# Row statistics moved from VectorE to ScalarE and the opening of an attention kernel put in another order

## The chip, the cores and the metric

The kernel runs on one core of a Trainium2 chip. The time is that of the device, in microseconds (us), for one launch. A core has five engines that work side by side, each through its own list of instructions in order: TensorE (PE in the profile, PEld for its weight loads), VectorE (DVE), ScalarE (ACT), GpSimd (POOL) and SyncE (SP), which here only issues DMAs. They wait for each other through semaphores.

## What is computed

Cross attention on a normalised input, with a residual, and behind it a transformer block with grouped-query attention over the four batches and a mixture of eight experts. The change touches only the opening of the first part:

```python
def _layernorm(x, axis=-1, eps=1e-05):
    m = jnp.mean(x, axis=axis, keepdims=True)
    v = jnp.var(x, axis=axis, keepdims=True)
    return (x - m) / jnp.sqrt(v + eps)
...
# B, S, D, H = (4, 512, 256, 16), DK = 16, 1024 context tokens
query = _rope(split_heads(q @ w_q.T))
key_ = _rope(split_heads(k @ w_k.T))
value = split_heads(v @ w_v.T)
scores = jnp.einsum('bhqd,bhkd->bhqk', query, key_) / np.sqrt(DK)
scores = jnp.where(mask[:, None, None, :] == 0, -10000.0, scores)
attn = jax.nn.softmax(scores, axis=-1)
...
x = x + _L0_xattn_ref(_layernorm(x, axis=-1), ctx_1024, ctx_1024, mask_BxS2_ik0, ...)
x = x + _L0_ffn_ref(_layernorm(x, axis=-1), ...)
```

x is (4, 512, 256), the context (4, 1024, 256), all in float32. Products are made exact enough by splitting both operands into a high and a low part (`_hi`, `_lo`) and adding three matmuls.

## The kernel before, in words

**Tiling.** The 2048 rows of x stand in SBUF as 16 tiles of 128 rows (`xt`, four to a batch). The attention of a batch goes in four quads of four heads; a quad has 8 groups, one for each 128 keys, so there are 128 groups in all. In a group TensorE computes scores for 4 heads (`score`, L974), ScalarE the exponentials (L643), and TensorE weighs the values (L989). Since the maximum of a row of scores has to be known ahead of its exponentials, each quad's scores are computed once more beforehand in the other orientation (`max`, L935: two matmuls of 49 rows into a `wide` bank) and VectorE reduces them (L781). There are 16 such maxima to a quad: 2 head pairs x 4 query tiles x 2 halves of the keys (`kh`). Then `nm` negates and joins them (L785 to L791), `mxt` turns them over (L940), ScalarE copies them to `mxp`, and SyncE's `load_max_rows` stores them as two more rows of `qst`.

**The order of the work.** `attention_order` writes one list of jobs; every engine walks it and does its own part of each job, so a place in the list fixes the order on all engines. The list `before` is the opening, up to the first group:

- ("rate", b): row statistics. VectorE's `statistics` does batch 0 at the very start, and batches 1 to 3 as ("rate", 1) behind the value projections of batch 0: 12 `bn_stats` (L700), 12 `bn_aggr` (L704), the variance plus epsilon (L706), then it waits for ScalarE's square root (L589) and makes `rstd` (L708) and `shift` (L711).
- ("xn", b, t): the normalised tile t, by ScalarE from batch 1 on (L608). ("xT", b): its transposes (L922), ScalarE's copy `xT_hi` (L637) and VectorE's subtraction `xT_lo` (L759). For batch 1 both stand in the opening, because its queries are projected from the second group on.
- ("c", b, g): GpSimd splits a half of the context (L521, L523). ("q"), ("k"), ("v"): projections (L849) and their evictions by ScalarE (L637); with an index at the end a job is a quarter of the work, 256 columns.
- ("rope", b, part): rotation of keys (part 0 and 1) or queries (part 2), by GpSimd or VectorE (L469 to L483).
- `first`, the 16 maxima of quad 0, upper half of the keys first: behind each of the first 12 stands one quarter job of batch 1, first the 8 of the keys, then 4 of the values. xT of batch 1 stands behind the eighth.
- Then `nm`, two value jobs, `mxt`, two maxima of quad 1, two value jobs, two more maxima; and then the groups. ScalarE loads the table for the exponential there (L660).

**Banks.** Maxima and transposes take turns on two `wide` banks, each freed by VectorE. Projections, `mxt` and scores go round in three `narrow` banks.

**SyncE's queue** is written by hand. Rotated pieces go to memory (`store_turned`, L353: `q_pieces` and `k_pieces`) and come back stacked for the heads (`load_queries` L374, `load_keys` L387). The first maximum waits for `quad_in`: the first two heads' queries and the upper half of their keys. A load waits for the landing of its store.

## Time and profile before

| | us |
|---|---|
| median of 3 runs | 776.78 |
| the three runs | 770.8, 776.78, 779.75 |
| the profiled execution | 778.03 |
| its span on the core | 776.2 |
| TensorE busy | 700.1 (90%) |
| VectorE busy | 559.5 (72%) |
| ScalarE busy | 494.4 (64%) |
| GpSimd busy | 355.3 (46%) |

### The profile page before, as it was taken

To read this page: it belongs to the slowest core of one execution; us is meant where nothing else is said; L and a number is where in the kernel's file an instruction comes from. 1 tells how busy PE (TensorE), PEld (TensorE's weight loads), DVE (VectorE), ACT (ScalarE), POOL (GpSimd) and SP (SyncE) were. 2 spreads that over 40 slices of the span, in tenths; PEclk is the share of its full clock that TensorE was granted. 3 is DMA by queue.
4 is the path that set the end of the run, shared out by engine and by line. 5 is a ranking of instruction groups with operands and counts; after the bars stand their busy time and mean duration, and the time that the engine had idled before them with its cause. 6 is when DMAs were issued, how large, how long until landed. Compare 5 with 4: busy or idle time off the path is not lost. (4 is left out here: it accounts for less than half of the span.)

```text
span 776.2 us, 13476 instructions
## 1 busy us (share of the span) xinstructions
PE 700.1 (90%) x4382; PEld 434.2 (56%) x4382; DVE 559.5 (72%) x919; ACT 494.4 (64%) x984; POOL 355.3 (46%) x262
## 2 busy tenths in 40 slices
PE   2379799999999999999999999889977789999996
PEld 2266444434344444444433433567766779999995
DVE  4995878888878878787988893367986435555553
ACT  2022367787777787878777778576646057677673
POOL 4857724880511096159668910000064703544444
PEclk9776699999999999999999999989987799999999
DMA  9575338667776474148967710089437636633321
GB/s 266 196 251 187 131 111 302 163 201 249 221 261 190 120 224 180 54 171 268 287 233 270 280 75 1 1 271 419 139 82 234 195 93 138 111 36 36 39 28 20
DMA packets 59719, 130.71 MB, mean 168 GB/s; under 512 B 8869, under 2 KB 26309, under 8 KB 58197
## 3 DMA queue, kind: packets, MB, share of 16 engines
q1 hardware_dynamic: 33364, 72.86, 27.9%
q0 software_dynamic: 16848, 35.95, 18.0%
q10 hardware_dynamic: 9440, 21.06, 9.2%
q8 instruction: 37, 0.61, 0.3%
q14 instruction: 30, 0.24, 0.1%
HBM read 80.80 MB, written 69.39 MB: 194 GB/s over the span
## 5 line engine op out<-in xcount | busy, mean ns | idle before, releaser
L781 DVE TENSOR_REDUCE mx<-wide 128x2 f32<-128x1024 f32 x256 | 307.3, 1222 | 62.5 <-PE wide L935 61.2
L643 ACT ACTIVATE probs<-narrow 128x512 f32<-128x512 f32 x492 | 265.6, 599 | 76.5 <-PE narrow L974 74.7
L974 PE MATMUL narrow<-qst,kst 51*128 51x512 f32 x492 | 186.5, 452 | 0.8 <-ACT probs L643 0.2
L935 PE MATMUL wide<-kst,qst 49*128 49x512 f32 x512 | 172.7, 466 | 9.0 <-DVE mx L781 6.4
L974 PEld LDWEIGHTS narrow<-qst,kst 51*128 51x128 f32 x492 | 79.8, 187 | 133.2 <-ACT probs L643 52.9
L989 PE MATMUL values<-probs,vaug 128*17 128x512 f32 x1024 | 136.4, 605 | 1.4 <-ACT probs L643 0.8
L1739 POOL DMA_INDIRECT out<-res,token x39 | 60.8, 1560 | 91.4 <-DMA out<-res,token 59.9
L935 PEld LDWEIGHTS wide<-kst,qst 49*128 49x128 f32 x512 | 71.3, 191 | 21.9 <-DVE mx L781 15.1
L1271 POOL DMA_DIRECT2D out<-xt x4 | 5.5, 1377 | 116.4 <-DVE xt L1466 116.4
L1764 ACT ACTIVATE h_hi<-narrow 128x512 fp32r<-128x512 f32 x39 | 23.4, 599 | 41.2 <-PE narrow L1844 41.2
L474 POOL TENSOR_TENSOR turn_b<-turn_a,tab 128x1024 f32<-128x1024 f32 x10 | 24.1, 2409 | 50.2 <-ACT turn_a L637 49.6
L1790 DVE TENSOR_TENSOR h_lo<-narrow,h_hi 128x512 fp32r<-128x512 f32 x39 | 27.0, 692 | 23.4 <-ACT h_hi L1764 23.4
L989 PEld LDWEIGHTS values<-probs,vaug 128*17 128x17 f32 x1024 | 17.0, 95 | 44.2 <-issue 27.0
L1278 POOL DMA_INDIRECT list_rows<-lists,rows_to x32 | 32.4, 1011 | 17.3 <-issue 8.5
L469 POOL TENSOR_SCALAR keep<-keep 128x512 f32<-128x512 int32 x7 | 13.6, 1945 | 54.1 <-ACT turn_a L637 50.8
L637 ACT ACTIVATE vaug<-narrow 128x256 f32<-128x256 f32 (+1 forms) x28 | 11.7, 416 | 41.8 <-PE narrow L849 40.9
L1786 DVE TENSOR_TENSOR y_lo<-y_full,y_hi 128x256 fp32r<-128x256 f32 x39 | 16.6, 425 | 29.1 <-ACT y_hi L1751 29.1
L1751 ACT ACTIVATE y_hi<-wide,lncol 128x128 fp32r<-128x128 f32 x78 | 36.3, 466 | 0.0
L1750 ACT ACTIVATE y_full<-wide,lncol 128x128 f32<-128x128 f32 x78 | 35.8, 459 | 0.1
L521 POOL CAST c_hi<-craw 128x1024 fp32r<-128x1024 f32 x5 | 5.2, 1039 | 57.1 <-DMA craw<-in_ctxT 36.1
L849 PE MATMUL narrow<-wv_hi,c_hi 128*128 128x256 f32 x64 | 17.5, 360 | 15.0 <-POOL wv_lo L486 15.0
L1835 PE MATMUL wide<-w_hi,y_hi 128*128 x78 | 28.2, 443 | 0.1
(291 smaller groups left out, 1371.6 us busy)
## 6 DMA issues: line engine op xcount, KB each, us to landing
list_rows<-in_w ACTq DMA_DIRECT2D x56, 342.0 KB, 5.5
kst<-k_pieces SPq DMA_DIRECT2D x14, 784.0 KB
k_pieces<-turn_a SPq DMA_DIRECT2D x16, 512.0 KB, 4.3
w_hi<-w_hi SPq DMA_DIRECT2D x16, 512.0 KB
w_lo<-w_lo SPq DMA_DIRECT2D x16, 512.0 KB
turn_a<-in_w POOLq DMA_DIRECT2D x11, 512.0 KB, 5.4
w_hi<-turn_b POOLq DMA_DIRECT2D x11, 512.0 KB, 2.9
w_lo<-turn_a POOLq DMA_DIRECT2D x11, 512.0 KB, 4.6
```

Of the source, the lines that this page charges most:

```text
L474: step(engine.tensor_tensor(z[:, :, :], a[:, :, :], cos, ALU.mult))
L643: nc.scalar.activation(probs[:, n % NP, :], score_bank(n), ACT.Exp, scale=DK ** -0.5).then_inc(exp_done, 1)
L781: last = nc.vector.tensor_reduce(mx[quad % 2][:, qt, :, hp, kh], slot[:, :, :], axis=AX.X, op=ALU.max)
L935: last = nc.tensor.matmul(slot[:, i, :], qst[u % 3][r:r + R_MAX, h, P * qt:P * qt + P], kst[u % 3][r:r + R_MAX, h, 512 * kh:512 * kh + 512 ...
L974: nc.tensor.matmul(score_bank(n), kst[u % 3][r:r + R_ALL, h, P * kt:P * kt + P], qst[u % 3][r:r + R_ALL, h, :], start=True, stop=True).the ...
L989: last = nc.tensor.matmul(values[32 * hq:32 * hq + DK + 1, :], vaug[b % 2][:, kt, h, :], probs[:, (4 * g + hq) % NP, :], start=kt == 0, st ...
L1278: pool.indirect_dma_start(list_dram, bass.IndirectOffsetOnAxis(rows_to[:, j, i, s:s + 1], 0), lists[j][:, i, s, :].bitcast(U32), None).the ...
L1739: pool.indirect_dma_start(out, bass.IndirectOffsetOnAxis(token[:, n:n + 1], 0), res[n % PIECES][:, :], None, bounds_check=TOKENS - 1, oob_ ...
L1750: nc.scalar.activation(yT[n % 2][:, k, :], y_banks[n % 2][:, k, :], ACT.Identity, **affine)
L1751: last = nc.scalar.activation(yT_hi[n % 2][:, k, :], y_banks[n % 2][:, k, :], ACT.Identity, **affine)
L1790: nc.vector.tensor_tensor(hT_lo[n % 2][:, :, :], h_banks[n % 2], hT_hi[n % 2][:, :, :].bitcast(F32), ALU.subtract).then_inc(h_lo_set, 1)
L1835: last = nc.tensor.matmul(up_banks[n % 2], a[n % 2][:, k, :], w[:, bass.ds(e, 1), k, :].rearrange("p e n -> p (e n)"), start=(i, k) == (0, ...
```

## The change

Four things in the opening, all of them order or place:

1. The statistics of batches 1 to 3 go to ScalarE, as a job ("sums", 1) behind the weight copies and ahead of the value projections of batch 0. For each of 12 tiles one pass sums the row (`accum_out`), one operation makes the negative means, and for each tile a second pass squares x plus this shift and sums. Each pass waits for the one before. The passes write their elements to a spare part of `attn`. VectorE keeps the variance, `rstd` and `shift` (`rest_of_statistics`). ScalarE's square root stays where ("rate", 1) stands.
2. ("xn", 1) goes behind the eighth key job, ("xT", 1) behind `mxt`.
3. The quarter jobs of batch 1 begin behind the third maximum and not behind the first.
4. SyncE stores the first half of the rotated keys behind the mask rows and the first queries' load, not ahead of them.

```diff
-    before += [("rate", 1), ("c", 1, 0), ("c", 1, 1)] + [("xn", 1, n) for n in range(QT)]
+    before += [("rate", 1), ("c", 1, 0), ("c", 1, 1)]
...
-        before += [j] + (keys + vals)[n:n + 1] * (n < 12) + [("rope", 1, 0)] * (n == 3) + [("rope", 1, 1)] * (n == 7) + [("xT", 1)] * (n == 7)
+        before += [j] + (keys + vals)[n - 2:n - 1] * (2 <= n < 14) + [("rope", 1, 0)] * (n == 5) + [("rope", 1, 1)] * (n == 9) + [("xn", 1, t) for t in range(QT)] * (n == 9)
...
         load_context(1, 0)
         store_turned(0, 2)
-        store_turned(0, 1)
         load_keep(1, 0)
         load_queries(0, slice(0, 2))
+        store_turned(0, 1)
         load_keys(0, slice(0, 2), (1,))
...
+            if kind == "sums":
+                for t in range(QT, NT):
+                    if t % QT == 0:
+                        act.wait_ge(x_in[t // QT], 16)
+                    nc.scalar.activation(attn[:, 3, :], xt[:, t, :], ACT.Copy, accum_out=sums[:, t:t + 1]).then_inc(act_step, 1)
+                    act.wait_ge(act_step, t - QT + 1)
+                n = NT - QT
+                nc.scalar.activation(shift[:, QT:], sums[:, QT:], ACT.Copy, scale=-1.0 / D).then_inc(act_step, 1)
+                act.wait_ge(act_step, n + 1)
+                for t in range(QT, NT):
+                    nc.scalar.activation(attn[:, 3, :], xt[:, t, :], ACT.Square, bias=shift[:, t:t + 1], accum_out=squares[:, t:t + 1]).then_inc(act_step, 1)
+                    act.wait_ge(act_step, n + 1 + t - QT + 1)
+                nc.scalar.activation(attn[:, 3, 0:1], shift[:, QT:QT + 1], ACT.Copy).then_inc(squares_set, 1)
+                return
...
-        def statistics(i, batches):
+        def rest_of_statistics():
+
+            dve.wait_ge(squares_set, 1)
+            nc.vector.tensor_scalar(varc[:, QT:], squares[:, QT:], 1.0 / D, EPS, ALU.mult, ALU.add).then_inc(var_set, 1)
+            dve.wait_ge(std_set, 2)
+            step(nc.vector.reciprocal(rstd[:, QT:], std[:, QT:]))
             settle()
+            nc.vector.tensor_tensor(shift[:, QT:], shift[:, QT:], rstd[:, QT:], ALU.mult).then_inc(shift_set, 1)
```

How the rows stand on the engines, from the program's order. ScalarE before, from its last weight copies to its last eviction ahead of the exponentials:

```order
L598 ACTIVATE wo_hi<-probs 128x512
L637 ACTIVATE vaug<-narrow 128x32x16 x4
L589 ACTIVATE std<-varc 128x12
L608 ACTIVATE xn<-xt,shift,rstd 128x256 x4
L637 ACTIVATE turn_a<-narrow 128x256 x8
L637 ACTIVATE xT_hi<-wide 128x1024
L637 ACTIVATE vaug<-narrow 128x16x16 x6
L637 ACTIVATE mxp<-narrow 8x512
L637 ACTIVATE vaug<-narrow 128x16x16 x2
```

and now (`turn_a` holds keys, `vaug` values, `stats` the sums):

```order
L614 ACTIVATE wo_hi<-probs 128x512
L596 ACTIVATE attn,stats<-xt 128x256 x12
L599 ACTIVATE shift<-stats 128x12
L602 ACTIVATE attn,stats<-xt,shift 128x256 x12
L604 ACTIVATE attn<-shift 128x1
L653 ACTIVATE vaug<-narrow 128x32x16 x4
L591 ACTIVATE std<-varc 128x12
L653 ACTIVATE turn_a<-narrow 128x256 x8
L624 ACTIVATE xn<-xt,shift,rstd 128x256 x4
L653 ACTIVATE vaug<-narrow 128x16x16 x6
L653 ACTIVATE mxp<-narrow 8x512
L653 ACTIVATE xT_hi<-wide 128x1024
```

The statistics' passes stand ahead of the first value evictions, the square root stays behind the fourth; `xn` moved behind the eight keys and `xT_hi` behind `mxp`.

SyncE before, from the store of the rotated queries to the first load of keys:

```order
L353 DMA q_pieces<-probs 128x2x512 x3
L353 DMA k_pieces<-turn_a 128x2x512
L353 DMA k_pieces<-turn_b 128x2x512
L353 DMA k_pieces<-turn_a 128x2x512
L342 DMA keep<-in_mask 128x512
L374 DMA qst<-q_pieces 48x1024 x2
L387 DMA kst<-k_pieces 49x2x512 x2
```

and now:

```order
L355 DMA q_pieces<-probs 128x2x512 x3
L344 DMA keep<-in_mask 128x512
L376 DMA qst<-q_pieces 48x1024 x2
L355 DMA k_pieces<-turn_a 128x2x512
L355 DMA k_pieces<-turn_b 128x2x512
L355 DMA k_pieces<-turn_a 128x2x512
L389 DMA kst<-k_pieces 49x2x512 x2
```

The three key stores moved behind three loads; the key load that waits for them still follows them.

TensorE before, from the last value projection of batch 0 on (`wide` banks hold maxima, `narrow` ones projections):

```order
L849 MATMUL narrow0<-wv_hi,c_lo1 128x256 x2
L935 MATMUL wide1<-kst0,qst0 128x512 x2
L849 MATMUL narrow1<-c_hi0,wk_hi 128x256 x2
L849 MATMUL narrow1<-c_lo0,wk_hi 128x256 x2
L849 MATMUL narrow1<-c_hi0,wk_lo 128x256 x2
L935 MATMUL wide0<-kst0,qst0 128x512 x2
L849 MATMUL narrow2<-c_hi0,wk_hi 128x256 x2
```

and now:

```order
L873 MATMUL narrow0<-wv_hi,c_lo1 128x256 x2
L959 MATMUL wide1<-kst0,qst0 128x512 x2
L959 MATMUL wide0<-kst0,qst0 128x512 x2
L959 MATMUL wide1<-kst0,qst0 128x512 x2
L873 MATMUL narrow1<-c_hi0,wk_hi 128x256 x2
L873 MATMUL narrow1<-c_lo0,wk_hi 128x256 x2
L873 MATMUL narrow1<-c_hi0,wk_lo 128x256 x2
L959 MATMUL wide0<-kst0,qst0 128x512 x2
```

Three maxima now come ahead of the first key projection. The third takes the bank of the first.

## Rows read from the trace of the kernel before

**Rows 1.** The page: busy tenths and granted TensorE clock in 40 equal slices.

```profile
PE   2379799999999999999999999889977789999996
...
PEclk9776699999999999999999999989987799999999
```

**Rows 2.** Busy time by stretches; the column behind POOL is the granted clock.

```profile
core 0: us, PE busy (x) PEld busy (x) DVE busy (x) ACT busy (x) POOL busy (x), PEclk, DMA share, GB/s
...
56.00:68.00 12.00, 12.00 (x45) 8.69 (x44) 7.47 (x7) 2.65 (x8) 8.10 (x4) 0.51 0.71 207
...
76.50:80.80 4.30, 2.88 (x15) 1.55 (x14) 3.62 (x4) 0.77 (x2) 2.38 (x2) 0.90 0.05 18
80.80:90.00 9.20, 8.10 (x33) 6.15 (x34) 6.86 (x7) 1.74 (x4) 8.97 (x5) 0.50 0.05 18
...
200.00:300.00 100.00, 98.81 (x656) 44.62 (x656) 82.36 (x87) 77.95 (x151) 37.80 (x21) 1.00 0.64 196
```

**Rows 3.** Timeline at the seam: start us, us, engine, instruction, idle time before it.

```profile
83.06 0.19 DVE L785 TENSOR_REDUCE nm<-mx 128x16 f32<-128x32 f32 x1
...
85.55 1.01 PE L940 MATMUL narrow<-ident,mh 128*8 128x128 f32 x4 [1.08 <-DVE mh L791]
...
86.49 1.22 PE L935 MATMUL wide<-kst,qst 49*128 49x512 f32 x4
...
92.33 1.77 ACT L643 ACTIVATE probs<-narrow 128x512 f32<-128x512 f32 x3
```

**Rows 4.** Timelines of ScalarE, VectorE and GpSimd around the statistics.

```profile
43.79 0.60 ACT L637 ACTIVATE vaug<-narrow 128x512 f32<-128x512 f32 x1 [21.74 <-PE narrow L849]
...
45.98 4.01 DVE L700 BATCH_NORM_STATS2 stats<-xt 128x6 f32<-128x256 f32 x12
...
49.09 0.60 ACT L637 ACTIVATE vaug<-narrow 128x512 f32<-128x512 f32 x1 [0.83 <-PE narrow L849]
...
50.89 2.36 POOL L523 TENSOR_TENSOR c_lo<-xn,c_hi 128x1024 fp32r<-128x1024 f32 x1
...
50.97 2.31 DVE L706 TENSOR_SCALAR varc<-mv 128x12 f32<-128x12 f32 x1
...
53.31 0.21 ACT L589 ACTIVATE std<-varc 128x12 f32<-128x12 f32 x1 [3.63 <-DVE varc L706]
...
53.91 3.48 DVE L781 TENSOR_REDUCE mx<-wide 128x2 f32<-128x1024 f32 x3
...
54.11 2.08 ACT L608 ACTIVATE xn<-xt,shift,rstd 128x256 f32<-128x256 f32 x4 [0.58 <-DVE shift L711]
```

**Rows 5.** Timeline of TensorE: maxima of two pairs at each clock.

```profile
61.38 0.79 PE L935 MATMUL wide<-kst,qst 49*128 49x512 f32 x2
...
63.69 0.79 PE L935 MATMUL wide<-kst,qst 49*128 49x512 f32 x2
...
76.48 0.55 PE L935 MATMUL wide<-kst,qst 49*128 49x512 f32 x2
...
77.87 0.99 PE L935 MATMUL wide<-kst,qst 49*128 49x512 f32 x4
```

**Rows 6.** ScalarE's groups by form: count, busy us and mean ns.

```profile
L608 ACT ACTIVATE xn<-xt,shift,rstd 128x256 f32<-128x256 f32 x12 | 6.9, 597 | 0.6 <-DVE shift L711 0.6
```

**Rows 7.** Timeline of SyncE's issues, and the first maximum's weight load.

```profile
39.45 0.76 SPq L353 DMA_DIRECT2D k_pieces<-turn_a  x1
...
41.45 1.62 SPq L374 DMA_DIRECT2D qst<-q_pieces  x2
...
44.04 1.58 SPq L387 DMA_DIRECT2D kst<-k_pieces  x2
...
49.85 0.18 PEld L935 LDWEIGHTS wide<-kst,qst 49*128 49x128 f32 x2 [1.00 <-DMA kst<-k_pieces]
```

**Rows 8.** The tile kst up to 100 us: issue to landing.

```profile
DMA to landing us min/median/max: 6.3/7.7/12.1
```

**Rows 9.** Timeline of the turned rows of batch 1 (TensorE, VectorE).

```profile
68.15 1.84 PE L922 MATMUL wide<-ident,xn 128*128 128x128 f32 x8
...
71.16 1.23 DVE L759 TENSOR_TENSOR xT_lo<-wide,xT_hi 128x1024 fp32r<-128x1024 f32 x1 [3.11 <-ACT xT_hi L637]
```

More of the change, by code:

```diff
@@ L55, in attention_order @@
     before = [("rate", 0), ("xn", 0), ("w", "q"), ("c", 0, 1), ("w", "k"), ("mask", 0), ("xT", 0), ("k", 0, 1, 0), ("k", 0, 1, 1), ("rope", 0, 1), ("c", 0, 0),
-              ("q", 0, 0), ("q", 0, 1), ("rope", 0, 2), ("k", 0, 0, 0), ("k", 0, 0, 1), ("rope", 0, 0), ("w", "v"), ("w", "o")]
+              ("q", 0, 0), ("q", 0, 1), ("rope", 0, 2), ("k", 0, 0, 0), ("k", 0, 0, 1), ("rope", 0, 0), ("w", "v"), ("w", "o"), ("sums", 1)]
     before += [("v", 0, g, n) for g in range(2) for n in range(2)]
-    before += [("rate", 1), ("c", 1, 0), ("c", 1, 1)] + [("xn", 1, n) for n in range(QT)]
+    before += [("rate", 1), ("c", 1, 0), ("c", 1, 1)]
     keys, vals = [[(kind, 1, n // 4, n // 2 % 2, n % 2) for n in range(8)] for kind in "kv"]
@@ L61, in attention_order @@
     for n, j in enumerate(first):
-        before += [j] + (keys + vals)[n:n + 1] * (n < 12) + [("rope", 1, 0)] * (n == 3) + [("rope", 1, 1)] * (n == 7) + [("xT", 1)] * (n == 7)
-    before += [("nm", 0), vals[4], vals[5], ("mxt", 0)] + maxes(1)[:2] + vals[6:] + maxes(1)[2:AHEAD]
+        before += [j] + (keys + vals)[n - 2:n - 1] * (2 <= n < 14) + [("rope", 1, 0)] * (n == 5) + [("rope", 1, 1)] * (n == 9) + [("xn", 1, t) for t in range(QT)] * (n == 9)
+    before += [("nm", 0), vals[4], vals[5], ("mxt", 0), ("xT", 1)] + maxes(1)[:2] + vals[6:] + maxes(1)[2:AHEAD]
     timed = []
@@ L138, in cross_attention @@
     std = sb("std", [P, NT])
+    sums, squares = stats[:, :, 0], stats[:, :, 2]
     rstd = sb("rstd", [P, NT])
@@ L185, in cross_attention @@
     values_prepared, filled = sem("values_prepared"), sem("filled")
+    act_step, squares_set = sem("act_step"), sem("squares_set")
     var_set, std_set, shift_set = sem("var_set"), sem("std_set"), sem("shift_set")
@@ L693, in settle, with statistics @@
             dve.wait_ge(dve_step, steps[0])
-        def statistics(i, batches):
-            for b in batches:
-                dve.wait_ge(x_in[b], 16)
-                for t in range(QT * b, QT * b + QT):
-                    step(nc.vector.bn_stats(stats[:, t, :], xt[:, t, :]))
-            settle()
-            tiles = slice(QT * batches[0], QT * batches[-1] + QT)
-            for t in range(tiles.start, tiles.stop):
+        def rest_of_statistics():
[3 more added lines that the diff above has]
+            step(nc.vector.reciprocal(rstd[:, QT:], std[:, QT:]))
+            settle()
+            nc.vector.tensor_tensor(shift[:, QT:], shift[:, QT:], rstd[:, QT:], ALU.mult).then_inc(shift_set, 1)
+        def statistics():
+            dve.wait_ge(x_in[0], 16)
+            for t in range(QT):
+                step(nc.vector.bn_stats(stats[:, t, :], xt[:, t, :]))
+            settle()
+            for t in range(QT):
                 step(nc.vector.bn_aggr(mv[:, t, :], stats[:, t, :]))
             settle()
-            nc.vector.tensor_scalar_add(varc[:, tiles], mv[:, tiles, 1], EPS).then_inc(var_set, 1)
-            dve.wait_ge(std_set, i + 1)
-            step(nc.vector.reciprocal(rstd[:, tiles], std[:, tiles]))
+            nc.vector.tensor_scalar_add(varc[:, 0:QT], mv[:, 0:QT, 1], EPS).then_inc(var_set, 1)
+            dve.wait_ge(std_set, 1)
+            step(nc.vector.reciprocal(rstd[:, 0:QT], std[:, 0:QT]))
             settle()
-            if i > 0:
-                nc.vector.scalar_tensor_tensor(out=shift[:, tiles], in0=mv[:, tiles, 0], scalar=-1.0, in1=rstd[:, tiles], op0=ALU.mult, op1=ALU.mult).then_inc(shift_set, 1)
         def masks():
@@ L721, in _ @@
             if kind == "rate":
-                statistics(j[1], [0] if j[1] == 0 else list(range(1, B)))
+                if j[1] == 0:
+                    statistics()
+                else:
+                    rest_of_statistics()
                 continue
```

## The prediction

> **What bounds the kernel now.** I read the page first. Its slices [rows 1] show TensorE busy nine tenths or more from the sixth to the 25th, at full clock; the slices ahead of them are thinner, and the second to fifth have a lowered clock. The table by stretches [rows 2] says the same with numbers: from 200 to 300 us TensorE is busy for 98.81 of 100 us at clock 1.00. So the attention loop is TensorE's, it neither waits for the opening nor can catch up with it, and a microsecond won or lost ahead of the first exponential is one at the end. I therefore follow the opening alone, up to the first exponential at 92.33 us [rows 3], and let that move carry through one for one.
>
> Then the timeline of the opening. VectorE ends its last rope block at 46.0 and goes straight into the twelve row statistics of batches 1 to 3, and it isn't free for the first maximum before 53.91 [rows 4]. Of the 7.9 us between, 4.0 are the statistics, 1.0 the aggregation (until 50.97), and 2.31 one tiny operation on 12 columns, which began while GpSimd was in its 2.36 us subtraction (50.89 to 53.25) and ended 0.03 us after it. ScalarE stands idle for 21.74 us before the first value eviction at 43.79.
>
> From there the order on TensorE is maximum, projection, maximum, projection. One such pair takes 63.69 - 61.38 = 2.31 us at the low clock and 77.87 - 76.48 = 1.39 at the high one [rows 5]; a maximum without a projection costs VectorE 3.48 / 3 = 1.16 [rows 4]. From 56 to 68 us TensorE is busy for the whole 12.00 us and has 0.51 of its clock, that is 1.2 GHz; from 76.5 to 80.8 the same kind of work has 0.90 and from 80.8 to 90 again 0.50 [rows 2]. The clock, 0.92 us a pair, is the largest term in the opening, and nothing in the change sets it directly.
>
> **The change part by part.**
>
> Statistics to ScalarE. VectorE loses 12 statistics and 12 aggregations (5.0 us) and keeps three operations on 12 columns. ScalarE gets 12 sums, 12 squares and two tiny operations between its weight copies and its value evictions. The nearest row is the normalisation of the same 128x256 tiles, 597 ns [rows 6]. Each pass waits for the one before it, so I take 0.65: 24 x 0.65 + 0.5 = 16.1 us from 22.05, done at 38.2. No row has a sum read-out beside an activation. Bounds: 0.5 (the pitch of four overlapped ones, 2.08 / 4 [rows 4]) ends at 34.6, and twice the row, 1.2, ends at 51.3. At 0.65 the 21.74 us of idle time cover it with 5 us over, so it costs nothing; from 0.9 us a pass on it delays the value evictions.
>
> VectorE's first step then is early, but its reciprocal waits for the square root, and that stands on ScalarE behind the fourth value eviction: 49.09 + 0.60, + 0.21 for the root [rows 4], then 0.5 for reciprocal and shift: ready at 50.4. The shift is now a product of two operands in SBUF, and GpSimd works from 50.89 to 53.25 there. If the shift queues behind that, as the variance did, VectorE is ready at 53.5. Bounds 50.4 and 53.5; both gain on 53.91.
>
> The Trainium skill, "SBUF — State Buffer", section "Who interferes with whom", says that a VectorE instruction with two SBUF inputs, or in a two-port mode, blocks on a GpSimd instruction that reads SBUF until that one ends. The trace agrees with it at the 2.31 us operation, and by this rule the moved chain can still be held, until 53.25, and the first reduction then comes at 53.4 in place of the 53.2 below, which adds 0.2 us to the sum.
>
> The reordered loads. SyncE issues mask rows, then the first queries, and only then the key store of the first half. Before, store issues ended at 40.21 and mask and queries at 43.07 [rows 7]; swapped, the store ends 2.86 us later, at 43.07 (at best not at all later, if both fit into waits). The key load waits for this store to land: before 44.04 - 40.21 = 3.83 us, and the keys were there 49.85 - 44.04 = 5.81 us after its issue. So keys at 43.07 + 3.83 + 5.81 = 52.7, where they were at 49.85 with 3.6 us of slack ahead of VectorE. This eats nearly the whole gain: first maximum on TensorE at 52.7, reduction at 53.2 (bounds 50.9 and 55.1, the latter with the median landing of 7.7 [rows 8]). Gain 0.7 us.
>
> The store of the second half and everything behind it on SyncE's queue shift by little: its key load waits for its own store, and its first use is the ninth maximum.
>
> Order of the pairs. Before, two projections ran between the first two maxima while VectorE was still busy, so they were free, and four maxima at the end stood alone. Now the first two and the last two stand alone, and 12 pairs follow without a break. The third maximum needs the bank of the first: 53.2 + 1.2 = 54.4. All pairs low: 12 x 2.31 = 27.7, to 82.1. All high: 12 x 1.39 = 16.7, to 71.1. In the profile about half of the pairs behind the first ran low. I take 5 low and 7 high, 21.3, to 75.7. That is more high ones than before had because the row is unbroken: before, the turned rows in the middle left VectorE idle for 3.11 us and TensorE waiting, the gap in which a clock can fall [rows 9]. The last two maxima: 0.5 for TensorE and 2 x 1.2: 78.6, against 83.06 before [rows 3], 4.5 earlier. Here the bubble in the middle is gone too; it was 1.84 us of transposes, and the next maximum but one waited for the subtraction that ended at 71.16 + 1.23 [rows 9].
>
> The normalisation moves on ScalarE behind the eighth key eviction: 2.08 us of work [rows 4], ahead of a value eviction. ScalarE has idle time after each eviction and TensorE has three banks to go round in, so I put it at nothing; without that cover one pair is some 1 us late.
>
> The turned rows at the seam. From the negated maxima to their transposition 2.49 us as before: 78.6 + 2.5 = 81.1. From there to the first exponential it was 92.33 - 85.55 = 6.78. Now the second maximum of the next quad needs the bank of the turned rows. Ahead of it stand 1.0 for the maxima's transposition, TensorE's 8 transposes (1.84 low [rows 9], half of that high), ScalarE's copy (between the end of the transposes, 69.99, and VectorE's start at 71.16: 1.17) and VectorE's 1.23: it starts 5.3 us (low) or 3.9 (high, where the first takes 0.6) after the start of the transposition. Before, it started at 86.49 + 0.61 = 87.1 [rows 3], 1.55 after it at the low clock, 0.9 at the high one. Cost 3.7 or 3.0, I take 3.3: 81.1 + 6.8 + 3.3 = 91.2, that is 1.1 us before 92.33. The load of the maxima's rows is hidden in this time.
>
> Sum: -1.1. The profiled execution took 778.03 us (776.2 of span and 1.8 around it), so 776.9; it stands 1.25 above the median of 776.78, whose three runs lie between 770.8 and 779.75. The profile is one draw of the clock and a dear one, so I take 776.0; the rivals' times are on the profile's own scale. About 1% (7.8 us) is what a measurement of this kernel can tell from no change, and this isn't near it.
>
> **The rivals.**
>
> Low clock throughout, the one on the slower side: its place is the row of 12 pairs, its price 0.92 a pair, and it decides from the seventh low pair on (2 x 0.92 = 1.8, more than the 1.1 gained with five). With 12: 82.1 + 3.1 = 85.2, transposed at 87.7, exponential at 87.7 + 6.8 + 3.7 = 98.2, 5.9 late: 783.9. For it: 56 to 68 us stayed at 0.51 in this very pattern, and TensorE now stands idle from 49.1 to 52.7 ahead of it. Against: the same pattern ran high at 76.5.
>
> High clock throughout: 71.1 + 2.9 = 74.0, transposed at 76.5, then 5.9 (the last two value projections 0.9 shorter) and 3.0: 85.4, 6.9 early: 771.1. The Trainium skill, "TensorE: Matmul & The Clock Gate", section "What's actually happening", says that being throttled is the default and that activity releases it; by that rule an unbroken row of work should run high. The 12.00 busy us at 0.51 speak against so simple a reading.
>
> The keys come later still: store and load meet other traffic. With the longest landing of a key load, 12.1 us [rows 8], in place of 5.81, the first maximum is 6.3 behind the forecast: 783.2. With the median, 1.9: 778.8. For it: the load of the queries now runs together with the store. Against: the store of the second half no longer runs beside the first key load.
>
> ScalarE's passes are long: at 1.2 us they end at 51.3, four evictions follow (2.4), root and two steps 0.7: VectorE ready at 54.4 and the first reduction 1.2 late: 778.1. Only if a read-out costs as much as the pass.
>
> **How the numbers follow.** Forecast (mixed clock) 0.42, own range 773 to 779; low throughout 0.16; high throughout 0.17; keys late 0.17; long passes 0.08. The range from 770.5 to 782 leaves out some of the low and of the late cases and the luckiest. Faster by over 1% (below 769.0) needs the high clock and a lucky block behind it: 0.08. Slower by over 1% (above 784.5) needs the low clock and late keys together: 0.07. Within 1%: 0.85.
>
> **What would show it.** In the profile after: VectorE's three small steps between 50 and 53.5 and no statistics there; ScalarE's 24 passes ended before 43.8, each at 0.6 to 0.7; a first maximum that waits for the key load and not for VectorE, at about 52.7; 12 pairs at either 2.3 or 1.4 with a count of each; a wait of the second maximum of the next quad for the turned rows, about 3 us; and a first exponential near 91. A loop that is less than 98% busy, or an end that moves by another amount than the first exponential, would make the whole way of reckoning wrong.

## The result, and the profile after

The changed kernel takes 777.61 us (median of 20 runs, 772.05 to 785.71), the kernel before 772.33 in the 20 runs beside it (763.39 to 780.24). The ratio is 1.0093, 95% interval 1.0067 to 1.012: slower, by a little under 1%. (The ratio leaves out runs over 1.5% above the fastest of their kernel; the medians of all runs give 1.0068.) The forecast was a gain of 1.1 us on the profiled run and 776.0 in all, which is no change that can be told. The number came near by luck, since two errors cancel: the kernel before is 4.4 us faster than its first three runs said, and the change costs 5 us where it was to gain one. The sign was missed.

The profile of the changed kernel looks, against the one shown of before, like a success. Its page [beside rows 1]:

```profile
PE   3269699999999999999999999889977689999996
...
PEclk9768889999999999999999999989997789999999
```

Its busy time by stretches [beside rows 2; the number behind POOL is the granted clock]:

```profile
56.00:68.00 12.00, 12.00 (x49) 8.50 (x49) 6.94 (x7) 2.30 (x6) 4.09 (x2) 0.60 0.71 184
68.00:80.80 12.80, 10.66 (x70) 7.84 (x69) 10.76 (x11) 5.42 (x13) 11.06 (x8) 1.00 0.39 159
80.80:90.00 9.20, 5.53 (x34) 3.34 (x32) 7.31 (x7) 5.54 (x10) 8.88 (x5) 0.97 0.46 175
...
200.00:300.00 100.00, 98.80 (x653) 44.09 (x651) 82.01 (x88) 78.42 (x152) 37.66 (x22) 1.00 0.64 192
```

The loop is as full as it was (98.80 of 100 us), and the opening ran higher in its clock than that of rows 2 did, 0.79 against 0.75 over the first 100 us.

The timeline around the statistics, ScalarE, VectorE, GpSimd and TensorE [beside rows 4 and 5]:

```profile
21.36 0.42 ACT L596 ACTIVATE attn<-xt 128x256 f32<-128x256 f32 x1 [0.81 <-DMA xt<-in_x]
21.69 0.19 ACT L596 ACTIVATION_READ_ACCUMULATOR attn<-xt 128x1 f32 x1
21.90 0.42 ACT L596 ACTIVATE attn<-xt 128x256 f32<-128x256 f32 x1
...
28.12 0.51 ACT L602 ACTIVATE attn<-xt,shift 128x256 f32<-128x256 f32 x1
28.53 0.19 ACT L602 ACTIVATION_READ_ACCUMULATOR attn<-xt,shift 128x1 f32 x1
28.75 0.51 ACT L602 ACTIVATE attn<-xt,shift 128x256 f32<-128x256 f32 x1
...
35.72 0.20 ACT L604 ACTIVATE attn<-shift 128x1 f32<-128x1 f32 x1
43.23 0.60 ACT L653 ACTIVATE vaug<-narrow 128x512 f32<-128x512 f32 x1 [7.30 <-PE narrow L873]
...
46.64 0.68 SPq L389 DMA_DIRECT2D kst<-k_pieces  x2
...
49.10 1.04 POOL L523 CAST c_hi<-xn 128x1024 fp32r<-128x1024 f32 x1
...
49.44 0.72 DVE L718 TENSOR_TENSOR shift<-shift,rstd 128x12 f32<-128x12 f32 x1
50.22 2.34 POOL L525 TENSOR_TENSOR c_lo<-xn,c_hi 128x1024 fp32r<-128x1024 f32 x1
51.93 1.22 PE L959 MATMUL wide<-kst,qst 49*128 49x512 f32 x4 [3.52 <-DMA kst<-k_pieces]
52.77 3.49 DVE L805 TENSOR_REDUCE mx<-wide 128x2 f32<-128x1024 f32 x3 [2.60 <-PE wide L959]
54.05 0.79 PE L959 MATMUL wide<-kst,qst 49*128 49x512 f32 x2 [0.90 <-DVE mx L805]
```

A pass is two entries, the elements (0.42 us for a sum, 0.51 for squares) and a read of the sum (0.19); one pass follows the next after 0.54 us (sums) and 0.63 (squares). All 24 and the small copy behind them are over at 35.92, and ScalarE still waits 7.30 us for the first values. VectorE is ready at 50.16, 2.6 us ahead of its first maximum, and it is TensorE that now waits, 3.52 us, for the keys.

The seam [beside rows 3]:

```profile
77.85 0.18 DVE L809 TENSOR_REDUCE nm<-mx 128x16 f32<-128x32 f32 x1
78.07 1.24 DVE L813 CAST mh<-nm 128x16 fp32r<-128x16 f32 x1
...
79.67 0.60 PE L964 MATMUL narrow<-ident,mh 128*8 128x128 f32 x4 [2.14 <-DVE mh L815]
80.10 1.04 PE L946 MATMUL wide<-ident,xn 128*128 128x128 f32 x8
...
82.30 1.23 DVE L783 TENSOR_TENSOR xT_lo<-wide,xT_hi 128x1024 fp32r<-128x1024 f32 x1 [2.78 <-ACT xT_hi L653]
...
83.58 0.50 PE L959 MATMUL wide<-kst,qst 49*128 49x512 f32 x2 [2.01 <-DVE xT_lo L783]
...
87.55 2.41 ACT L659 ACTIVATE probs<-narrow 128x512 f32<-128x512 f32 x4
```

The first exponential comes at 87.55 against 92.33 of rows 3, 4.8 us earlier, and the span is 773.9 against 776.2. Two profiles, one of each kernel, say "faster by 2 us"; twenty runs of each say "slower by 5". (The exponential gained 4.8 us and the span 2.3, so half of the gain was lost behind it; more on this below.) What resolves this is how much one run differs from the next, and by what.

**The measure used below.** Each run's result lists its span and its mean granted clock. As TensorE's levels are 1.2 and 2.4 GHz, a run with clock c and span s spent 2(1 - c)s microseconds at 1.2 GHz; I call that its low time. The profile of before had 0.939 over 776.2 us: 95 us. Over the runs of the 18 kernels below (206 runs, each set around its own mean) time and low time go together with a correlation of 0.90, at 0.35 us of time for a us of low time. The 20 runs of the changed kernel had 88 us of it in the mean.

### The profile page after: what moved, and what is told of

Read it like the earlier page. It is cut to its first block and busy times, and to the rows that moved or that the text cites. A ratio compares the mean times of both kernels' runs of the same rounds, so it can differ in the third digit from the quotient of the medians.

```text
span 773.9 us, 13504 instructions
## 1 busy us (share of the span) xinstructions
PE 696.5 (90%) x4382; PEld 429.7 (56%) x4382; DVE 554.3 (72%) x895; ACT 507.8 (66%) x1034; POOL 355.9 (46%) x262
## 5 line engine op out<-in xcount | busy, mean ns | idle before, releaser
L653 ACT ACTIVATE turn_a<-narrow 128x256 f32<-128x256 f32 (+1 forms) x38 | 15.0, 395 | 25.2 <-PE narrow L873 24.0
```

## The experiments

Eighteen kernels, each timed in five rounds beside the kernel before on the same chip, up to 12 runs against 19 to 35. "us" and "low" are differences of the means of all runs to those of before; the standard error of a "us" is 1.0 to 1.9, of a "low" 2.4 to 5.2. One run of before took 1045.95 us at a clock of 0.558; it stood beside after_fill, mix, mix_fill and u_loads and is left out of their "us" and "low", which it would move by -7.7 us and -24 us. Runs of before differ by chip (means of 770.6 to 777.6 us), so each kernel is compared with those beside it.

| kernel | ratio [95%] | us | low |
|---|---|---|---|
| before_again | 1.0002 [0.9963, 1.0042] | +0.1 | -0.3 |
| after_again | 1.0078 [1.0046, 1.0111] | +6.2 | +11.5 |
| a_stats | 0.9987 [0.9946, 1.0027] | -1.3 | +1.6 |
| a_loads | 1.0022 [0.9983, 1.006] | +1.3 | +0.9 |
| a_turned | 1.001 [0.9964, 1.0056] | +2.5 | +7.2 |
| a_keys | 0.9989 [0.9953, 1.0025] | -0.2 | -1.3 |
| u_loads | 1.0078 [1.0039, 1.0116] | +5.2 | +14.1 |
| u_turned | 1.004 [1.0002, 1.0078] | +4.6 | +10.5 |
| u_keys | 1.0046 [1.0002, 1.009] | +7.5 | +17.4 |
| after_fill | 1.005 [1.0019, 1.0081] | +2.4 | -7.9 |
| after_mid | 1.0103 [1.0052, 1.0154] | +7.0 | +8.5 |
| mix | 0.9965 [0.9934, 0.9996] | -2.9 | -3.3 |
| mix_again | 0.9911 [0.9872, 0.995] | -4.5 | -6.2 |
| mix_fill | 0.9981 [0.9951, 1.0012] | -3.1 | -5.0 |
| mix_loads | 1.0065 [1.0028, 1.0103] | +4.5 | +7.8 |
| mix_loads_fill | 0.9947 [0.9913, 0.998] | -3.5 | -7.9 |
| mix_turned | 0.998 [0.9939, 1.0021] | -1.5 | -1.2 |
| mix_keys | 1.0011 [0.9972, 1.0049] | +0.5 | +2.3 |

A straight line through these 18 has a slope of 0.43 us per us of low time (correlation 0.87); I use it as the price of low time. It is a fit and not a measurement of a cause; with the 0.35 from run to run each share below is a fifth smaller.

The traces say where the differences lie. From 46 to 110 us the low time is 9.0 us in mix_loads_fill, 12.3 in mix, 24.0 in before_again, 30.7 in after_again, 41.0 in mix_loads and 54.6 in u_keys. Behind 110 us it lies between 28.7 and 43.5 in all twenty profiles, in no order that follows the kernels.

The expectations name theories by letters: S, the turned rows at the seam cost the time; K, TensorE's waits in the opening lower its clock; L, the late keys cost by themselves; M, the clock is low because the turned rows left the middle; A, the passes on ScalarE hurt elsewhere; R and N, the result repeats or was chance.

**One part alone.** In the kernel before: a_stats has the statistics on ScalarE, a_loads the order of loads, a_turned the normalisation behind the eighth maximum and the turned rows at the seam, a_keys the quarter jobs from the third maximum on.

```diff
 # a_loads
-        store_turned(0, 1)
         load_keep(1, 0)
         load_queries(0, slice(0, 2))
+        store_turned(0, 1)
 # a_keys (a_turned: xn at n == 7, xT behind mxt)
-  before += [j] + (keys + vals)[n:n + 1] * (n < 12) + ...
+  before += [j] + (keys + vals)[n - 2:n - 1] * (2 <= n < 14) + ...
```

a_stats:

> The kernel before with part 1 alone: row statistics of batches 1 to 3 by ScalarE, everything else in the old order. Theory S (the turned rows at the seam cost the time, part 1 gains): VectorE is ready at 50.4 in place of 53.9 and the keys are there at 49.9, so about 3 us faster. Theory K (what costs is TensorE waiting in the opening, which puts more of it at 1.2 GHz): the wait of 2.6 us ahead of the third maximum goes too, so 3 us and up to 3 more, 3 to 6 us faster. Theory A (the passes on ScalarE hurt elsewhere, which I don't believe since they end at 35.9): no gain.

a_loads:

> The kernel before with part 4 alone: the store of the first half of the keys behind the mask rows and the first queries. The keys come at about 52 in place of 49.9, VectorE is not ready before 53.9. Theory S: nothing, within 1 us. Theory K: TensorE, which did a maximum and two projections between 49.9 and 52.6, waits 3 us there and does them against VectorE's first reductions: 1 to 3 us slower.

a_turned:

> The kernel before with part 2 alone: xn of batch 1 behind the eighth key job, its transposes at the seam behind mxt. Theory S: 2 to 3 us gained in the middle, 3 to 4 lost at the seam, and TensorE's waits there (2.1 and 2.0 us) put the first groups of the loop at 1.2 GHz: 3 to 5 us slower. Theory K: gain in the middle and loss at the seam cancel: within 1.5 us.

a_keys:

> The kernel before with part 3 alone: quarter jobs of batch 1 from the third maximum on, the turned rows still behind the eighth of them. Theory K: TensorE has nothing to do from 50.8 to 55.2 and the first pairs run at 1.2 GHz, two more pairs are bound by TensorE: 3 to 5 us slower. Theory S: two pairs of 1.39 or 2.31 in place of two free ones: 0.5 to 2 us slower.

All four lie within 0.3% of no change, and each interval includes 1. So a_stats missed its 3 to 6 us of gain and a_keys its loss under either theory, while a_loads (+1.3 us) and a_turned (+2.5, between the two theories) decide nothing. The sum of the four, +2.3 us with an error of about 3, isn't the +6 of the whole, so either the parts act together or the errors hide it. Two of the traces show stalls. The first row is a_stats, where the normalisation still stands behind the statistics and waits on ScalarE for GpSimd's split context, with the key evictions behind it; the second, in a fence of its own, is a_keys, where two maxima alone meet a VectorE that is still at its statistics:

```profile
56.28 0.50 PE L873 MATMUL narrow<-c_hi,wk_hi 128*128 128x256 f32 x2 [1.47 <-ACT turn_a L653]
```

```profile
54.53 0.80 PE L935 MATMUL wide<-kst,qst 49*128 49x512 f32 x2 [4.21 <-DVE mx L781]
```

**The whole again, one part undone, and the kernel before against itself.**

```diff
 # u_loads: store_turned(0, 1) ahead of load_keep again
 # u_turned: xn behind ("rate", 1), xT in the middle
-  ... [("xn", 1, t) for t in range(QT)] * (n == 9)
+  ... [("xT", 1)] * (n == 9)
 # u_keys
-  before += [j] + (keys + vals)[n - 2:n - 1] * (2 <= n < 14) + ...
+  before += [j] + (keys + vals)[n:n + 1] * (n < 12) + ...
```

after_again:

> The changed kernel once more, unchanged, beside the kernel before, on a chip where the four parts alone came out within 0.3% of before. Theory R (the 0.9% of the first comparison is a property of the whole: parts add up or meet): 1.007 to 1.011 again. Theory N (the spread of single executions, some 16 us from the lowest to the highest, and the chip decide, the structure being worth a microsecond or two): 0.997 to 1.005. In the trace I expect the first exponential between 86 and 93 us in either case.

before_again:

> The kernel before against itself, for the error of the comparison and for a second trace of its opening. Ratio within 0.4% of 1. Its first profile had 44.4 us at 1.2 GHz ahead of the first exponential, the traces of the kernels with one part had 27 to 38; if that profile was a dear draw, this one shows fewer than 40 and a first exponential before 90.

u_turned:

> The changed kernel with part 2 undone: xn behind the rates and xT in the middle again, now behind the eighth key job of the later row (tenth maximum). If the turned rows at the seam are what costs (theory S), it is 2 to 4 us faster than the changed kernel, so 1.000 to 1.005 of before where the changed one has 1.007; under theory N the two are alike.

u_keys:

> The changed kernel with part 3 undone: quarter jobs from the first maximum on, xn behind the eighth, xT at the seam. Theory K (TensorE's wait of 3.5 us for the keys and the bound of 12 pairs, at 1.2 GHz for the first of them): with two projections under VectorE's first two reductions 1 to 3 us faster than the changed kernel. Theory N: alike.

u_loads:

> The changed kernel with part 4 undone: the key store of the first half goes first again. In all four traces with the new order TensorE waited 3.5 to 4.6 us for the keys and the clock was at 1.2 GHz when the maxima began; in those with the old order the wait was 0.4 to 2.6. Theory L (late keys, directly): 1 to 2 us faster than the changed kernel, ratio to before 1.004 to 1.006. Theory K (the wait lowers the clock, and the pairs then stay low): 3 to 6 us faster, ratio 1.000 to 1.004. Theory S (seam): 1.006 or more.

The result repeats on another chip (1.0078), and the comparison has no bias (1.0002). The new thing is the low time: +11.5 us for the whole, which at 0.43 is 4.9 of its +6.2. And undoing a single part doesn't take it back: the low time stays 10 to 17 us up. By the ratios u_turned and u_keys recover some of the loss (1.004 and 1.0046 against 1.0078, with intervals that overlap), inside what theory S allowed u_turned, and u_loads nothing at all: 1.0078, where K had 1.000 to 1.004 and only S had 1.006 or more. But the seam alone doesn't explain 14.1 us more of low time. The value of u_keys is the least sure: its +7.5 us rest on the half of its runs that its ratio leaves out, and the other six give +3.5 us and +5.0 of low time. Its profile, one of the long runs, shows what the low clock looks like at its worst, busy time by stretches:

```profile
52.00:64.00 12.00, 11.61 (x42) 8.30 (x42) 6.13 (x5) 1.53 (x4) 2.27 (x2) 0.50 0.64 179
64.00:76.00 12.00, 12.00 (x42) 8.37 (x42) 6.13 (x5) 4.22 (x10) 11.54 (x8) 0.50 0.52 183
76.00:88.00 12.00, 9.66 (x36) 6.70 (x34) 9.53 (x8) 1.54 (x4) 8.23 (x4) 0.50 0.13 55
88.00:100.00 12.00, 9.47 (x37) 6.62 (x37) 5.75 (x6) 4.36 (x7) 8.27 (x5) 0.50 0.57 220
```

TensorE went low right ahead of the row and stayed at 1.2 GHz for 54.6 us on end, though it was busy for 12.00 of the 12 us from 64 to 76. Being dense didn't lift the clock there. The rows of the other traces that were entered low came back high behind 5 low pairs (the changed kernel) or 9 (after_again), so a row that is entered low is low for a part of its length that differs from run to run.

The profile of the kernel before in before_again, a run of 767.9 us of span, is what rows 2 to 4 look like on a more usual draw, by stretches and in the timeline:

```profile
56.00:68.00 12.00, 10.90 (x66) 8.12 (x64) 9.00 (x9) 4.31 (x11) 8.12 (x4) 0.93 0.74 194
68.00:80.80 12.80, 11.34 (x64) 8.22 (x62) 11.00 (x13) 2.90 (x7) 7.36 (x6) 0.87 0.38 151
```

```profile
51.26 1.91 DVE L706 TENSOR_SCALAR varc<-mv 128x12 f32<-128x12 f32 x1
...
53.79 2.35 DVE L781 TENSOR_REDUCE mx<-wide 128x2 f32<-128x1024 f32 x2
...
76.98 0.19 DVE L785 TENSOR_REDUCE nm<-mx 128x16 f32<-128x32 f32 x1
...
78.14 0.60 PE L940 MATMUL narrow<-ident,mh 128*8 128x128 f32 x4
78.67 0.73 PE L935 MATMUL wide<-kst,qst 49*128 49x512 f32 x4
...
82.86 1.28 ACT L643 ACTIVATE probs<-narrow 128x512 f32<-128x512 f32 x2
```

From 56 to 68 us the clock is 0.93 where rows 2 have 0.51, and the first exponential is at 82.86 (expected: before 90), 9.5 us ahead of rows 3, with the same program.

**Dummy work in the wait.** If the clock falls because TensorE stands idle for the keys, then work of no use in that wait must bring it back, though it adds to TensorE's load.

```diff
 # after_fill, ahead of the first maximum's wait
+ if (quad, hp, qt, kh) == (0, 0, 0, 1):
+     for _ in range(26):
+         nc.tensor.matmul(slot[:, 0, 0:P], ident[:, :], ident[:, :], start=True, stop=True)
```

after_fill:

> The changed kernel with 26 dummy matmuls of 128 columns into the bank of the first maximum, ahead of its wait for the keys: some 3.4 us of work in a wait of 3.5 to 4.6. No work of the kernel moves. Theory K: the maxima begin at 2.4 GHz, the row of pairs runs at 1.39 us a pair, and it is 3 to 6 us faster than the changed kernel (ratio to before 0.999 to 1.004, mean granted clock back from 0.945 to 0.950 or more). Theories L and S: no change or 0 to 1 us slower, ratio 1.006 to 1.009.

The low time falls from 11.5 above the kernel before's to 7.9 below, and the difference from +6.2 to +2.4 us. The dummies in the trace of after_fill, and the first maxima behind them:

```profile
48.62 5.97 PE L955 MATMUL wide<-ident 128*128 128x128 f32 x52
54.51 0.73 PE L962 MATMUL wide<-kst,qst 49*128 49x512 f32 x4
```

They ran 2.5 us past the keys (52 or so in the other traces of this order), so the +2.4 may be what I overfilled by. The ratio, 1.005, is just outside theory K's 0.999 to 1.004 and just below the 1.006 of the others, and its interval overlaps that of after_again; it is the low time, 19 us less, that speaks for K. So work ahead of the row raises the clock; which part of the change lowers it isn't shown.

**A mixed version.** mix is the changed kernel with the old loads, the old quarter jobs and the turned rows in the middle, but with the normalisation behind the fifth key job, which takes away a_stats' stall. mix_fill adds 12 dummies ahead of the first maximum.

```diff
 # mix
+  ... [("xn", 1, t) for t in range(QT)] * (n == 4) + [("xT", 1)] * (n == 7)
```

mix:

> Part 1 with nothing else but the normalisation moved behind the fifth key job: old loads, keys from the first maximum on, transposes in the middle. In the trace with part 1 alone ScalarE stood at the normalisation (it waits for GpSimd's split of the context) with a key eviction behind it, and TensorE waited 1.5 us for the bank. All theories: VectorE ready at 50.4 and no such wait, so 2 to 4 us faster than before, ratio 0.995 to 0.997; under theory K up to 6 us (0.992).

mix_fill:

> The same with 12 dummy matmuls (1.6 us at the high clock) ahead of the wait for the keys, which is 0.4 to 2.6 us there. Theory K: the clock doesn't fall ahead of the first pair, 0 to 3 us faster than without. The others: alike or 0.5 us slower.

mix is faster than both kernels, 0.9965, inside the expected 0.995 to 0.997; mix_fill is no better (0.9981). The wait that its dummies fill was 0.71 us in mix's trace and 1.93 in mix_again's, against 2.8 us of dummies.

**Each part on top of mix, and dense work in the middle.** These ask which part brings the low clock. after_mid is the changed kernel with 8 dummies ahead of the ninth maximum, where the transposes used to be.

```diff
 # mix_loads: the loads of a_loads.   mix_turned: xn at n == 7, xT behind mxt
 # mix_keys: quarter jobs from n == 2, xn at n == 6, xT at n == 9
 # after_mid
+ if (quad, hp, qt, kh) == (0, 0, 0, 0):
+     for _ in range(8): nc.tensor.matmul(...)
```

mix_loads:

> The best version so far (statistics on ScalarE, normalisation behind the fifth key projection, turned rows in the middle, old loads) with the changed kernel's order of loads. Theory K (TensorE's longer wait for the keys ahead of the row leaves the row longer at 1.2 GHz): TensorE waits 3 to 5 us in place of 1 to 2.6, some 5 to 10 us more at 1.2 GHz per run, 2 to 5 us slower than that version, ratio about 1.000 to 1.003. Theory L (only the keys' delay counts): later by the 1 to 2 us of the first maximum, with no more low time: 0.998. Theory M (only the turned rows' place matters for the clock): low time as in that version, below the kernel before's.

mix_turned:

> The same version with the turned rows moved to the seam and the normalisation behind the eighth key projection. Theory M (with the turned rows out of the middle the row stays longer at 1.2 GHz): low time 5 to 10 us above the kernel before's, and the seam 3 us longer, ratio 1.001 to 1.005. Theory S (only the seam's 3 us): low time as before, ratio 0.999 to 1.001. Theory K: low time as before.

mix_keys:

> The same version with the key projections from the third maximum on. Two maxima alone at the start, two alone at the end. Theories M and K alike: no more low time than the kernel before has, ratio 0.995 to 0.999. If the order of the pairs itself keeps the clock low (rival), low time 5 to 10 us more and a ratio above 1.000.

after_mid:

> The changed kernel with 8 dummy matmuls (some 2 us of dense work, no result used) ahead of the ninth maximum, where the kernel before had its transposes. Theory M: the low time falls from 12 us above the kernel before's to at most 5 above, and the difference from 6 us to at most 4 in spite of the 2 us added. Theory K: low time stays 10 to 14 us above, difference 6 to 8 us.

mix_loads goes from -2.9 to +4.5 us and from -3.3 to +7.8 of low time, by one store moved on SyncE; its ratio, 1.0065, is above the 1.000 to 1.003 of theory K and far above the 0.998 of L. mix_turned and mix_keys can't be told from the kernel before (for mix_keys, 0.995 to 0.999 was expected). after_mid keeps 8.5 us of low time (error 2.8, six runs), above theory M's 5 and below K's 10; together with mix_turned, which has the turned rows out of the middle and no more low time (-1.2, where M had +5 to +10), it speaks against M but doesn't exclude it.

The eight kernels with the statistics on ScalarE are all combinations of the other three parts (mix none, the three just named one each, u_keys, u_turned and u_loads two, after_again three; the place of the normalisation differs a little). The mean of the four with a part less the four without it:

| part | us | low |
|---|---|---|
| order of loads | +5.4 | +8.8 |
| turned rows at the seam | +2.7 | +6.1 |
| quarter jobs from the third maximum | +2.2 | +4.4 |

(us with a standard error of 1.0, low of 2.7.) By the ratios of the same eight the parts cost 0.49%, 0.25% and 0.38%, so only the first place of the loads is sure. The effects don't add: on mix the loads cost 7.4 us, but on u_loads, which has the other two already, only 1.0 more (after_again). The other two matter mostly together: mix_turned -1.5, mix_keys +0.5, but both, u_loads, +5.2. So either the loads or the other two together bring the low clock, and in the kernel as it was changed taking back the loads alone would gain next to nothing.

**Is it the idle wait or the late keys?** mix_loads with 12 dummies in the wait, and mix once more, on another chip.

mix_loads_fill:

> That version with the changed kernel's order of loads, and 12 dummy matmuls in TensorE's wait for the keys (some 2.8 us, inside a wait of 3.9). Theory K: the low time falls from 8 us above the kernel before's to at most 3 above, the difference from +4.5 us to between -2 and +1. Theory L (late keys cost by themselves, the clock's part is luck): low time and difference stay, +4 to +6 us.

mix_again:

> The best version once more (statistics on ScalarE, old order of loads and of projections, turned rows in the middle, normalisation behind the fifth key projection). If it is truly faster than the kernel before: ratio 0.995 to 0.999, some 3 us, with a low time 0 to 5 us below. If the first comparison was luck: 1.000 within 0.004.

The clearest pair of the study. The kernel mix_loads, TensorE's timeline at the wait and its stretches:

```profile
46.55 0.40 PE L873 MATMUL narrow<-wv_hi,c_lo 128*128 128x256 f32 x2
50.81 0.80 PE L959 MATMUL wide<-kst,qst 49*128 49x512 f32 x2 [3.86 <-DMA kst<-k_pieces]
```

```profile
47.00:50.70 3.70, 0.00 (x0) 0.00 (x0) 0.96 (x2) 0.69 (x2) 3.62 (x3) 0.94 0.94 337
50.70:52.00 1.30, 1.19 (x4) 0.75 (x5) 0.36 (x1) 0.00 (x0) 0.41 (x1) 0.50 0.65 251
...
52.00:64.00 12.00, 12.00 (x44) 8.69 (x44) 6.62 (x6) 3.12 (x8) 3.33 (x2) 0.50 0.67 173
```

And mix_loads_fill, the same two views:

```profile
46.57 2.84 PE L955 MATMUL wide<-ident 128*128 128x128 f32 x24
50.42 0.49 PE L962 MATMUL wide<-kst,qst 49*128 49x512 f32 x2 [1.01 <-DMA kst<-k_pieces]
```

```profile
47.00:50.70 3.70, 2.69 (x24) 2.40 (x22) 1.00 (x2) 0.47 (x2) 3.62 (x3) 1.00 1.00 363
50.70:52.00 1.30, 1.30 (x10) 0.96 (x8) 1.04 (x1) 0.14 (x1) 0.24 (x1) 1.00 0.47 183
...
52.00:64.00 12.00, 11.39 (x72) 8.32 (x70) 9.55 (x9) 6.19 (x14) 7.43 (x4) 1.00 0.69 174
```

The keys come at the same moment (50.8 and 50.4). Ahead of them TensorE is idle for 3.86 us in the one and for 1.01 in the other; the one falls to 0.50 at the end of its idle time and gets 44 matmuls into the 12 us behind it, the other keeps 1.00 and gets 72. Over the runs: +4.5 us and +7.8 low against -3.5 and -7.9. The two pairs of means come from different chips; against mix_again, on the same chip and with the early keys, mix_loads_fill is 1.1 us slower (error 1.9). So late keys cost little or nothing by themselves here; most of their price is the clock. mix_again is faster than the kernel before a second time, 0.9911 [0.9872, 0.995], more than the 0.995 to 0.999 expected. Its own profile, by the way, shows the row low (0.50 from 52 to 64 us), in a set of runs with 6 us less low time than the kernel before: one profile doesn't tell a kernel's clock.

**What stays open.** In the kernels with the statistics still on VectorE, pauses as long did no visible harm over the runs: a_loads waited 3.30 us for the keys (low +0.9), a_keys 4.21 us for VectorE (low -1.3). In a_loads the first maximum behind the wait was still at the high clock (0.50 us) and the second, 1.6 us later, at the low one (0.79), so the clock doesn't always fall within the pause. With errors of 3 us on each low time, a_loads and mix_loads differ by 6.9 +- 4.3, so this may be chance, or the place of the pause may matter. And why u_loads, where TensorE waits 0.41 us for the keys and 1.48 for VectorE, goes low as often as it does isn't explained; dummies there weren't tried.

## Why the prediction was right and wrong

**What bounds the kernel: right in kind, not one for one.** The loop is at 98.80%, and the end follows the first exponential, but loosely. From there to the end of the span it was 683.9 us in the profile of before, 686.4 after and 685.0 in before_again, and over the twenty profiles from 681.8 (after_again) to 691.4 (a_stats); a line through them gives 0.72 us of span for a us of the first exponential (error 0.11). This is the sign that the prediction itself named, "an end that moves by another amount". A forecast of -1.1 us that stops at the first exponential is smaller than this scatter. Where the rest is made up or lost isn't shown.

**Statistics to ScalarE: right.** 0.54 and 0.63 a pass against 0.65, over at 35.92 against 38.2, all hidden. VectorE ready at 50.16 against 50.4. The rule of the Trainium skill ("SBUF — State Buffer", "Who interferes with whom"), by which a VectorE instruction with two SBUF inputs contends with a GpSimd instruction that reads SBUF, agrees with the trace: the shift took 0.72 us and ended at 50.16, with GpSimd's cast at 50.14. The old one, on the same 12 columns and also with two inputs in SBUF, ran in before_again behind GpSimd's work and took 0.17:

```profile
53.70 0.17 DVE L711 SCALAR_TENSOR_TENSOR shift<-mv,rstd 128x12 f32<-128x12 f32 x1
```

So it wasn't the number of inputs that changed, as the prediction has it, but what ran beside the shift. It came ahead of the subtraction, so the 53.25 that I weighed didn't come.

**Reordered loads: the walk right, the consequence missed.** Keys at 51.93 against 52.7, TensorE's wait 3.52 us. I booked this as a loss of slack that VectorE no longer needed. Its larger price, shown on mix (mix_loads against mix_loads_fill), is the idle time it makes of TensorE ahead of the row of pairs.

**Order of the pairs: right on this draw.** Third maximum at 54.05 against 54.4; behind it exactly 5 low and 7 high pairs, from one maximum to the next 2.30 and 1.34 us; negated maxima at 77.85 against 78.6. That five was a guess from rows 2 that happened to be drawn: luck. The same program had nine low in after_again, and its relatives have anything from none (mix_loads_fill) to all of them (u_keys).

**The turned rows at the seam: right.** Forecast +3.0 at the high clock, and the second maximum 3.9 us behind the maxima's transposition. Measured: 83.58 - 79.67 = 3.9, and from that transposition to the first exponential 7.88 us against 4.72 in before_again, +3.2. The first exponential came 3.7 us before the forecast 91.2 since the seam ran at 1.00 and not at the low clock of rows 3.

**The step that failed** is "the clock ... is the largest term in the opening, and nothing in the change sets it directly", with the comparison that was built on it. Two faults, of about equal size:

- The change does set it. I wrote that "TensorE now stands idle from 49.1 to 52.7 ahead of it" as a point for the low rival, and priced the change as if the pairs were dealt by chance. It brings 11.5 us more of low time in after_again, an estimated 4.9 us of the +6.2 by the slope of 0.43 (4.0 by that of 0.35). The other 1.3 would be the seam less the statistics' small gain: mix and mix_again, at equal clock by the slope of 0.43, are 1.5 and 1.8 us faster than before (-2.9 + 0.43 x 3.3, -4.5 + 0.43 x 6.2). This split is worked out and wasn't measured by itself. The rival "low clock throughout", with 0.16, gave 783.9, 5.9 above the dear profile and so 6 above the 777.8 measured in the mean; it isn't that the pairs are always low, only more often. Of the other rivals, the late keys and the long passes didn't come, and the high clock throughout did in mix_loads_fill, where something keeps TensorE busy ahead of the row.
- I set the walk of the changed kernel, with a middling clock, against one profiled run of the kernel before, whose clock was far down (95 us low against 74 to 80 in its runs in the mean), and called the difference a gain of 1.1. I had seen it was dear and took off 0.9; it stood 5.4 above the mean of 772.6. The expected "4.5 earlier" of the negated maxima came from there: against before_again, at 76.98, the changed kernel's 77.85 isn't earlier at all.

The rule of the Trainium skill that I weighed ("TensorE: Matmul & The Clock Gate", "What's actually happening": throttled by default, released by activity) agrees with mix_loads_fill against mix_loads. The stretches of u_keys, 12.00 us busy at 0.50, don't agree with it as it stands, and there the measurement decides.

## What to carry to other kernels

Where the clock moves between two levels, a transfer that comes later than TensorE's last work can cost more by what runs behind it at half speed than by the wait: on mix a wait of 3.86 us went with +4.5 us and a filled one with -3.5. Before you give away slack there, try to keep TensorE busy up to a dense stretch, with useful work or even with dummies; a_loads and u_loads warn that not every pause costs and not every low stretch has one ahead of it. Don't set a forecast against one profile: read the granted clock of every run, and compare kernels by means of many, or walk both at the same clock. And don't carry a move of some us in the opening to the end one for one without looking how much the rest scatters (here by 10 us). Test parts of a change on a version where the rest is sound, not only alone and undone: here neither showed what the loads do, and the combinations did, with the finding that the effects don't add.

## What was unexpected of the hardware

- TensorE stayed at 1.2 GHz for 54.6 us on end in u_keys, though busy from 64 to 76 us without a gap.
- In mix_loads the clock was at 0.50 when work began again behind 3.86 idle us; in mix_loads_fill it was at 1.00 behind 2.84 us of dummies and 1.01 idle. But in a_loads it was still high behind 3.30 idle us, and in before_again low behind 2.55.
- Each 128x128 float32 dummy was recorded as two matmuls, 0.115 us each at the high clock (5.97 us for 52). A dummy so took 0.23 us, where I had counted on 0.13.
- A ScalarE pass with a sum is two instructions, the read of 0.19 us among them, and a chain in which each pass waits for the one before costs 0.54 us a pass, hardly more than the 0.52 (2.08 / 4, rows 4) of normalisations of the same tile that don't wait for each other.
- The runs of one program differ by 2% (763.4 to 780.2 us for the kernel before), and over the 206 runs most of such a spread goes with the time at 1.2 GHz. About half of the low time of a run lies behind the opening (43.5 of 95 us in the profile of before).
